# Three instead of four additions per step on GpSimd in a decoder scan kernel; slots 16 and 17 become two sums of TensorE

## The chip, the cores and the metric

The kernel runs on one core of one Trainium2 chip. The metric is the time of one execution on the device in microseconds (us), the median of several runs. The core has four engines that compute, each with its own queue of instructions, and they meet only at semaphores: TensorE (PE; its weight loads are listed as PEld), VectorE (DVE), ScalarE (ACT) and GpSimd (POOL). SyncE (SP) only starts transfers here. An engine works through its queue in order: an instruction that waits holds up everything behind it.

## The reference, cut to what matters

Sixteen sequences of 224 tokens and 512 features go through a Mamba layer, a pooled cross layer and a mixture of eight experts, with a layer norm after each. The change touches only the recurrence of the first layer:

```
deltaA = exp(delta[..., None] * A)
deltaBu = delta[..., None] * Bm[:, :, None, :] * xc[..., None]
# scan over the tokens, for 1024 channels x 16 states
h = dA * h + dBu
y = einsum('bdn,bn->bd', h, c)          # sum over the 16 states
y = (y + xc * Dp) * silu(z)
```

## The kernel before, in words

The program has three parts: a short beginning (to about 75 us), sixteen **steps**, one for each sequence (to about 1925 us), and the experts (from about 1990 us). Steps 2 to 11 are the body of a loop that does two steps a turn; steps 0, 1 and 12 to 15 are written out.

A step cuts the recurrence of one sequence into 32 **slots**: eight blocks of 128 channels (KB) times four groups of four states (Q). A slot is a tile of 128 channels by 4 states by 224 tokens = 128x896. Each slot passes through these instructions:

- POOL, L954: the input u = dx * B, written into a buffer of the ring `u`.
- ACT, L806: four exponentials, the decays, into one of two PSUM halves (`ring`).
- DVE, L1235: the scan. For 25 slots its result stays in `ring`; for the seven slots of POOLED = (1, 5, 9, ..., 25) it goes into the slot's buffer of `u`.
- the product with C: DVE, L1244, for the 25 slots; POOL, L959, for the seven. POOL does the product of slot s behind the L954 of slot s + 2.
- PE, L1540: the **sum** of a slot, four matmuls of the product with the identity, which add the four states into the PSUM bank of y. The trace shows a float32 matmul as two records, so a sum is "x8" there.

For the slots in ADDED POOL does one thing more: behind the product of slot s it adds the product of slot s - 1 into it (L965). PE then leaves out slot s - 1 and does one sum for both:

```
if s + 1 in ADDED:                                        # L1536, PE
    return
product_made(pe, b, s)
...
last.then_inc(sum_done, 2 if s in ADDED else 1)           # L1542
```

The ring `u` has five buffers up to slot 19 and four from slot 20 on (`s % 5 if s < 20 else s % 4`). POOL may write slot s (L954) only when PE has summed the slot that had this buffer before; it waits for `sum_done` (L949). So slot 21 waits for the sum of slot 16, slot 22 for that of 17, slot 25 for that of 21, slot 26 for that of 22, slot 27 for that of 23, slot 30 for that of 26. Before the change slot 16's buffer is given back only by the shared sum of 16 and 17.

Beside the 32 slots each engine does **side work** of the neighbouring sequences: PE projects the next sequence (L1368; a group "x24" is twelve matmuls of it), projects its time steps (L1379: dt0 to dt3), forms outputs (L1391, L1407, L1415), patches (L1423) and routing; ACT turns dt3 into terms (L579 to L584) of which DVE makes a correction (L1078, corr3); POOL makes the time steps (L888 to L895), normalised rows (L939), context (L933) and the scatter (L921). Tables (PE_AT, DVE_AT, ...) name the slot behind which each part stands. On PE, behind slot 15 stand twelve projection matmuls of the next gate (z0 and half of z1); behind slot 17 the patches (L1423); behind slot 20 twelve more projection matmuls and a transposition; behind 21 dt2; behind 25 dt3. DVE gets to corr3 behind the scan of slot 28.

Of the kernel before, what the change touches and what calls it, by code (L numbers as in the profile page):

```python
# [14 lines left out]
def build_decoder(nc, t):  # L15
# [42 lines left out]
    with ctx:  # L58
# [191 lines left out]
        def apart(eng):  # L250


            eng.sem_inc(wait_kept, 1)
# [89 lines left out]

        POOLED = tuple(range(1, SLOTS - Q, 4))
        MADE = SLOTS - len(POOLED)
        ADDED = (5, 9, 13, 17)
        made = lambda s: s + 1 - sum(p <= s for p in POOLED)
        pooled = lambda s: sum(p <= s for p in POOLED)

# [530 lines left out]
        def _(pool):  # L880
# [63 lines left out]
            def body(b, par):  # L944
                def main(s):
# [10 lines left out]
                    if s - 2 in POOLED:  # L956
                        q = (s - 2) % Q
                        pool.wait_ge(scan_done, b * SLOTS + (s - 1))
                        nc.gpsimd.tensor_tensor(u[:, u_of[s - 2]], u[:, u_of[s - 2]], bc[:, 1, q * QN:(q + 1) * QN, :], ALU.mult  # L959
                                                ).then_inc(pooled_ready if s - 2 not in ADDED else multiplied, 1)  # L960
                    if s - 2 in ADDED:
                        pool.wait_ge(multiplied, b * len(ADDED) + (ADDED.index(s - 2) + 1))
                        apart(pool)
# [377 lines left out]
        def _(pe):  # L1341
# [185 lines left out]
            def body(b, par):  # L1527
                def main(s):
# [3 lines left out]
                    if q == 0:  # L1532
                        if k % 2 == 0:
                            pe.wait_ge(skip_ready, b * PAIRS + (k // 2 + 1))
                            apart(pe)
                    if s + 1 in ADDED:  # L1536
                        return
                    product_made(pe, b, s)
                    for i in range(QN):
                        last = nc.tensor.matmul(o, ident, u[:, u_of[s], i, :], start=False, stop=(q == Q - 1 and i == QN - 1),  # L1540
                                                skip_group_check=True)
                    last.then_inc(sum_done, 2 if s in ADDED else 1)  # L1542

# [149 lines left out]
```

## Time and profile before

| what | value |
|---|---|
| time, median of 3 runs | 2677.05 us (2675.32 to 2677.08) |
| the profiled execution's own time | 2675.47 us |
| its span, first to last instruction | 2673.7 us |
| busy in the span | PE 2429.7, PEld 2054.5, DVE 2122.7, POOL 1786.1, ACT 1753.4 us |
| mean granted clock of TensorE | 0.954 |

Busy time is the time in which the engine had an instruction running. In a group of rows, "[0.57 <-POOL arena L959]" behind an instruction says that its engine sat idle for 0.57 us just before it, and that this instruction of POOL ended last of what it waited for. Records of matmuls overlap a little, so the distance from one start to the next tells more than a duration. PEclk is the granted clock as a share of full speed. "issue" is time in which the profile shows no wait.

### The profile page before, as it was taken

The numbers are of one execution on the slowest core, as the hardware profiler recorded it, in microseconds if no ns is written. First come the engines' busy times: TensorE is split into PE (matmuls) and PEld (weight loads), VectorE is DVE, ScalarE is ACT, GpSimd is POOL, SyncE is SP. The second block draws the span as 40 slices with busy tenths as digits, with TensorE's granted clock in tenths as the row PEclk, the third lists the DMA queues.
The fourth block names the chain that finished last, engine by engine and source line by source line (L and its number), as shares of the span: only waits on it lengthen the run. The fifth ranks groups of instructions, "written<-read, shape, count | busy, mean of one in ns | idle before, by whom it ended". The sixth has DMA issues, their size and how long they took to land.

```text
span 2673.7 us, 36163 instructions
## 1 busy us (share of the span) xinstructions
PE 2429.7 (91%) x11168; PEld 2054.5 (77%) x11168; DVE 2122.7 (79%) x2360; ACT 1753.4 (66%) x4011; POOL 1786.1 (67%) x1044
## 2 busy tenths in 40 slices
PE   5588999999999999999999999996869999999997
PEld 5576877777787787877777787774649999989896
DVE  5898999999999999999999999998733444444442
ACT  4676888888888887888888778887543333333331
POOL 0798999999999999999999999998610100000100
PEclk8799999999999999999999899998879999999998
DMA  7114202022120211202022120211052333333420
GB/s 226 62 49 154 80 12 90 15 84 76 29 88 19 83 47 59 87 12 91 15 83 74 31 87 18 76 42 56 25 173 95 122 131 119 122 121 125 142 81 18
DMA packets 90922, 208.63 MB, mean 78 GB/s; under 512 B 7743, under 2 KB 16575, under 8 KB 90499
## 3 DMA queue, kind: packets, MB, share of 16 engines
q1 hardware_dynamic: 81506, 184.61, 21.3%
q0 software_dynamic: 5120, 14.21, 1.7%
q10 hardware_dynamic: 4096, 7.34, 0.9%
q8 instruction: 103, 1.69, 0.3%
q14 instruction: 97, 0.79, 0.1%
HBM read 176.69 MB, written 29.98 MB: 77 GB/s over the span
## 4 chain that ended last, share of the span: by engine, by line
PE 36%; POOL 31%; issue 16%; DVE 12%; DMA 3%; ACT 1%; POOLq 0%; DVEq 0%; SPq 0%; ACTq 0%
POOL arena L954 20%; PE work L1555 12%; PE ring L1555 11%; POOL arena L959 6%; PE y L1540 5%; DVE ring L1235 4%; PE work L1368 3%; DVE arena L1070 2%; DVE arena L1244 2%; PE work L1391 1%; PE work L1407 1%; POOL arena L965 1%; POOL arena L892 1%; POOL arena L890 1%; POOL arena L888 1%
## 5 line engine op out<-in xcount | busy, mean ns | idle before, releaser
L954 POOL TENSOR_TENSOR arena<-arena 128x896 f32<-128x896 f32 x512 | 1058.3, 2089 | 56.8 <-PE y L1540 41.4
L806 ACT ACTIVATE ring<-arena,small 128x224 f32<-128x224 f32 x2048 | 795.4, 436 | 190.0 <-DVE arena L1244 150.4
L1540 PE MATMUL y<-arena,cst_sb 128*128 128x224 f32 x3584 | 779.7, 370 | 113.9 <-POOL arena L965 67.4
L1235 DVE TENSOR_TENSOR_SCAN ring<-ring,arena 128x896 f32<-128x896 f32 x400 | 809.4, 2024 | 57.9 <-POOL arena L954 39.6
L1540 PEld LDWEIGHTS y<-arena,cst_sb 128*128 128x128 f32 x3584 | 696.9, 199 | 192.0 <-POOL arena L965 75.4
L978 POOL DMA_INDIRECT out<-res,ids x32 | 44.7, 1395 | 642.0 <-DVE mst L1292 559.5
L1368 PE MATMUL work<-arena 128*128 128x224 f32 x1984 | 421.2, 370 | 19.8 <-DVE arena L1070 13.3
L1244 DVE TENSOR_TENSOR arena<-ring,arena 128x896 f32<-128x896 f32 x400 | 433.4, 1083 | 5.5
L1368 PEld LDWEIGHTS work<-arena 128*128 128x128 f32 x1984 | 393.6, 201 | 33.2 <-DVE arena L1070 17.8
L1307 DVE SCALAR_TENSOR_TENSOR hidden_lo<-work,hidden_hi 128x448 fp32r<-128x448 f32 x128 | 80.0, 625 | 345.8 <-ACT hidden_hi L856 345.8
L856 ACT ACTIVATE hidden_hi<-work 128x448 fp32r<-128x448 f32 x128 | 69.7, 544 | 370.3 <-PE work L1555 370.3
L1235 DVE TENSOR_TENSOR_SCAN arena<-ring,arena 128x896 f32<-128x896 f32 x112 | 225.7, 2015 | 21.4 <-POOL arena L954 15.5
L959 POOL TENSOR_TENSOR arena<-arena 128x896 f32<-128x896 f32 x112 | 233.7, 2087 | 13.0 <-DVE arena L1235 12.8
L1391 PE MATMUL work<-arena 128*112 128x512 f32 x496 | 220.6, 593 | 0.0
L1555 PE MATMUL ring<-hidden_hi,weights_hi 128*128 128x448 f32 x512 | 190.0, 371 | 0.0
L1555 PE MATMUL work<-xe_hi,weights_hi 128*128 128x448 f32 x512 | 188.4, 368 | 1.3 <-DVE xe_lo L1270 1.3
L1555 PE MATMUL work<-xe_lo,weights_hi 128*128 128x448 f32 x512 | 188.0, 367 | 0.0
L1555 PE MATMUL work<-xe_hi,weights_lo 128*128 128x448 f32 x512 | 187.9, 367 | 0.0
L1555 PE MATMUL ring<-hidden_hi,weights_lo 128*128 128x448 f32 x512 | 187.6, 366 | 0.0
L1555 PE MATMUL ring<-hidden_lo,weights_hi 128*128 128x448 f32 x512 | 187.5, 366 | 0.0
L1391 PEld LDWEIGHTS work<-arena 128*112 128x112 f32 x496 | 88.1, 178 | 102.4 <-issue 101.7
L1257 DVE TENSOR_TENSOR weights_lo<-weights,weights_hi 128x2048 fp32r<-128x2048 f32 x64 | 146.1, 2286 | 1.2 <-ACT weights_hi L820 1.2
(194 smaller groups left out, 3340.8 us busy)
## 6 DMA issues: line engine op xcount, KB each, us to landing
weights<-in_w SPq DMA_DIRECT2D x64, 1024.0 KB, 7.1
arena<-bc_rows SPq DMA_DIRECT2D x128, 448.0 KB, 4.4
arena<-in_ctx SPq DMA_DIRECT2D x16, 896.0 KB, 5.8
expert_rows<-x2e SPq DMA_DIRECT2D x1, 7224.0 KB, 31.8
xrow<-expert_rows SPq DMA_DIRECT2D x8, 903.0 KB, 12.0
arena<-in_xT SPq DMA_DIRECT2D x16, 448.0 KB, 6.3
arena<-in_x SPq DMA_DIRECT2D x16, 448.0 KB, 3.6
out<-arena ACTq DMA_DIRECT2D x32, 224.0 KB, 2.3
```

The lines of the kernel that those rows point to most:

```text
L806: last = nc.scalar.activation(decays[s % 2][:, i * L:(i + 1) * L], delta[:, k, :], ACT.Exp, scale=a_neg[:, n:n + 1])
L856: nc.scalar.activation(r32(h_hi[:, f % HR, :]), h_bank[f % 2][:, 0:CAP], ACT.Relu).then_inc(hid_hi, 1)
L954: nc.gpsimd.tensor_tensor(u[:, u_of[s]], dx[:, k:k + 1, :].to_broadcast([P, QN, L]), bc[:, 0, q * QN:(q + 1) * QN, :], ALU.mult).then_inc( ...
L959: nc.gpsimd.tensor_tensor(u[:, u_of[s - 2]], u[:, u_of[s - 2]], bc[:, 1, q * QN:(q + 1) * QN, :], ALU.mult).then_inc(pooled_ready if s - 2 ...
L1235: nc.vector.tensor_tensor_scan(states, h, u_flat[:, u_of[s], :], 0.0, ALU.mult, ALU.add).then_inc(scan_done, 1)
L1244: nc.vector.tensor_tensor(u[:, u_of[s]], h.rearrange("p (n l) -> p n l", n=QN), bc[:, 1, q * QN:(q + 1) * QN, :], ALU.mult).then_inc(p_rea ...
L1257: nc.vector.tensor_tensor(r32(lo), w, hi, ALU.subtract).then_inc(ready, 1)
L1307: nc.vector.scalar_tensor_tensor(r32(h_lo[:, f % HR, :]), h_bank[f % 2][:, 0:CAP], 0.0, h_hi[:, f % HR, :], ALU.max, ALU.subtract).then_in ...
L1368: last = nc.tensor.matmul(bank[:, i * L:(i + 1) * L], w_in[:, c, o:o + P], xn[:, c, :], start=(c == 0), stop=(c == DC - 1))
L1391: last = nc.tensor.matmul(bank[0:H, 0:D], gate[:, 1 - par, k, h * H:(h + 1) * H], w_out[:, k, :], start=(k == 0), stop=(k == KB - 1))
L1540: last = nc.tensor.matmul(o, ident, u[:, u_of[s], i, :], start=False, stop=(q == Q - 1 and i == QN - 1), skip_group_check=True)
L1555: last = nc.tensor.matmul(out, r32(a), r32(b), start=(first and k == 0), stop=(stop and k == n - 1))
```

## The change

ADDED loses its last member. POOL no longer adds slot 16 into slot 17; PE sums slot 16 and slot 17 one after the other, each from its own buffer, and each sum gives its own buffer back. Nothing else is edited; the products, the scans and the side work stay.

```diff
@@ -343,7 +343,7 @@
         POOLED = tuple(range(1, SLOTS - Q, 4))
         MADE = SLOTS - len(POOLED)
-        ADDED = (5, 9, 13, 17)
+        ADDED = (5, 9, 13)
         made = lambda s: s + 1 - sum(p <= s for p in POOLED)
         pooled = lambda s: sum(p <= s for p in POOLED)
```

PE, around slot 16 of a step that is written out (the sum of slot 15 and twelve projection matmuls stand first; L1423 are the patches behind slot 17, and the last row holds the sums of 18, 19 and 20):

```order
 L1540 MATMUL y<-arena,cst_sb 128x224 x4
 L1368 MATMUL work<-arena 128x224 x12
-L1540 MATMUL y<-arena,cst_sb 128x224 x4
+L1540 MATMUL y<-arena,cst_sb 128x224 x8
 L1423 MATMUL work<-cst_sb,mask_b 112x224 x2
 L1540 MATMUL y<-arena,cst_sb 128x224 x12
```

Behind the projection stands one sum more, four matmuls; everything behind it on PE comes four matmuls later.

POOL in the same part of a step, before (L954 x4 are slots 16 to 19, L959 and L965 product and addition of slot 17, the next L954 x4 slots 20 to 23, L959 the product of slot 21, L921 the scatter):

```order
L954 TENSOR_TENSOR arena<-arena 128x896 x4
L959 TENSOR_TENSOR arena<-arena 128x896
L965 TENSOR_TENSOR arena<-arena 128x896
L954 TENSOR_TENSOR arena<-arena 128x896 x4
L959 TENSOR_TENSOR arena<-arena 128x896
L954 TENSOR_TENSOR arena<-arena 128x896
L921 DMA expert_rows<-x2e,slot_i 3584x516 x2
```

and after:

```order
L954 TENSOR_TENSOR arena<-arena 128x896 x4
L959 TENSOR_TENSOR arena<-arena 128x896
L954 TENSOR_TENSOR arena<-arena 128x896 x4
L959 TENSOR_TENSOR arena<-arena 128x896
L954 TENSOR_TENSOR arena<-arena 128x896
L921 DMA expert_rows<-x2e,slot_i 3584x516 x2
```

One addition is gone between slot 19's and slot 20's input; the order is otherwise the same. The queues of DVE and ACT are unchanged.

## Rows read from the trace of the kernel before

**Rows 1.** The page: the chain that ended last, by engine.
```profile
PE 36%; POOL 31%; issue 16%; DVE 12%; DMA 3%; ACT 1%; POOLq 0%; DVEq 0%; SPq 0%; ACTq 0%
```
**Rows 2.** Windows of step 8 and step 9: length, busy (count) by engine, PEclk, DMA, GB/s.
```profile
1006.50:1118.60 112.10, 105.52 (x485) 86.86 (x484) 109.17 (x120) 92.86 (x225) 106.76 (x64) 0.98 0.18 55
1118.60:1235.00 116.40, 110.93 (x497) 90.39 (x497) 111.04 (x119) 96.30 (x240) 110.52 (x64) 0.97 0.19 61
```
**Rows 3.** Groups by line, whole span: busy, mean ns of one, idle before.
```profile
L1540 PE MATMUL y<-arena,cst_sb 128*128 128x224 f32 x3584 | 779.7, 370 | 113.9 <-POOL arena L965 67.4 <-DVE arena L1244 29.6 <-POOL arena L959 13.0
...
L965 POOL TENSOR_TENSOR arena<-arena 128x896 f32<-128x896 f32 x64 | 133.4, 2084 | 14.5 <-POOL arena L959 14.3 <-DVE arena L1244 0.2
```
**Rows 4.** Waits, whole span: us in total, times, longest.
```profile
POOL arena L954 <- PE y L1540: 41.4, 45, 3.2
DVE ring L1235 <- POOL arena L954: 39.6, 29, 8.3
```
**Rows 5.** Timeline of POOL, step 8: start, us, what [idle before]; slots 17, 21-23, 25-27.
```profile
1074.26 2.08 POOL L965 TENSOR_TENSOR arena<-arena 128x896 f32<-128x896 f32 x1 [0.24 <-POOL arena L959]
...
1078.63 6.19 POOL L954 TENSOR_TENSOR arena<-arena 128x896 f32<-128x896 f32 x3 [0.24 <-PE y L1540]
...
1091.31 6.18 POOL L954 TENSOR_TENSOR arena<-arena 128x896 f32<-128x896 f32 x3
```
**Rows 6.** Timeline of PE, step 8: projection, sum 17, patches, sums 22-23, sum 25.
```profile
1072.22 4.81 PE L1368 MATMUL work<-arena 128*128 128x224 f32 x24 [0.16 <-DVE slot_i L1140]
1076.87 1.68 PE L1540 MATMUL y<-arena,cst_sb 128*128 128x224 f32 x8
1078.38 0.92 PE L1423 MATMUL work<-cst_sb,mask_b 112*112 112x224 f32 x4
...
1091.18 3.29 PE L1540 MATMUL y<-arena,cst_sb 128*128 128x224 f32 x16
...
1099.59 1.78 PE L1540 MATMUL y<-arena,cst_sb 128*128 128x224 f32 x8 [0.57 <-POOL arena L959]
```
**Rows 7.** Timeline of DVE: first scan of step 9, and its corr3.
```profile
1118.60 2.03 DVE L1235 TENSOR_TENSOR_SCAN ring<-ring,arena 128x896 f32<-128x896 f32 x1 [1.09 <-POOL arena L954]
...
1219.17 0.60 DVE L1078 SCALAR_TENSOR_TENSOR arena<-arena,work 128x448 f32<-128x448 f32 x1
```
**Rows 8.** Timeline of PE, step 9: projection, sum 17, sums 22-23.
```profile
1186.09 4.81 PE L1368 MATMUL work<-arena 128*128 128x224 f32 x24
1191.30 1.78 PE L1540 MATMUL y<-arena,cst_sb 128*128 128x224 f32 x8 [0.40 <-POOL arena L965]
...
1205.72 3.29 PE L1540 MATMUL y<-arena,cst_sb 128*128 128x224 f32 x16
```
**Rows 9.** Timeline of POOL, step 9: the addition, then slots 20-23.
```profile
1189.16 2.08 POOL L965 TENSOR_TENSOR arena<-arena 128x896 f32<-128x896 f32 x1 [0.24 <-POOL arena L959]
1191.20 8.23 POOL L954 TENSOR_TENSOR arena<-arena 128x896 f32<-128x896 f32 x4
```
**Rows 10.** Timeline of ACT, step 9: the last term of dt3.
```profile
1218.55 0.54 ACT L584 ACTIVATE arena<-work 128x448 f32<-128x448 f32 x1
```
**Rows 11.** Timeline of POOL, step 1: slot 25.
```profile
288.27 2.09 POOL L954 TENSOR_TENSOR arena<-arena 128x896 f32<-128x896 f32 x1 [1.47 <-PE y L1540]
```
**Rows 12.** Timeline of PE, step 0: projection behind slot 15, sum 20.
```profile
151.22 4.70 PE L1368 MATMUL work<-arena 128*128 128x224 f32 x24
...
163.18 1.78 PE L1540 MATMUL y<-arena,cst_sb 128*128 128x224 f32 x8 [0.49 <-DVE arena L1244]
```
**Rows 13.** Timeline of DVE, step 15: scans 20 and 30.
```profile
1884.85 2.03 DVE L1235 TENSOR_TENSOR_SCAN ring<-ring,arena 128x896 f32<-128x896 f32 x1 [1.48 <-POOL arena L954]
...
1912.72 2.03 DVE L1235 TENSOR_TENSOR_SCAN ring<-ring,arena 128x896 f32<-128x896 f32 x1 [0.36 <-POOL arena L954]
```
**Rows 14.** Timeline of PE, step 3: the projection behind slot 15.
```profile
499.60 6.08 PE L1368 MATMUL work<-arena 128*128 128x224 f32 x24
```
**Rows 15.** Timeline of POOL, step 3: slots 21-23.
```profile
507.28 6.18 POOL L954 TENSOR_TENSOR arena<-arena 128x896 f32<-128x896 f32 x3 [3.19 <-PE y L1540]
```

## The prediction

> **What bounds the kernel now.** I read the page's chain first, then windows by step, then who waits for whom, then the engines' timelines around slots 16 to 27 of two neighbouring steps. The chain gives 36% to PE, which also has the experts, and 31% to POOL [rows 1]; within the steps most of it runs over POOL. Taken alone that says: POOL is the bound, take work from it. The windows say something narrower: in step 8 (112.1 us) DVE is busy 109.2, POOL 106.8 and PE 105.5 us [rows 2]. No engine has 7 us to spare, and PE, where the work goes, is as full as POOL, where it comes from. So the question is which wait ends last at the place of the change, and who is late behind it. Both directions of waiting exist: POOL's L954 waited 41.4 us for sums of PE in all, and the scans that write ring waited 39.6 us for POOL [rows 4].
>
> **What goes and what comes.** Sixteen additions go, one a step. An addition is 2.08 us, with a wait of 0.24 for POOL's own product before it [rows 3, 5]: 2.3 us a step on POOL, 37 us in all. Sixteen sums come, four matmuls each. Behind the projection the sum of 17 starts at 1076.87 and the next instruction at 1078.38 [rows 6]: 1.51 us a step on PE, 24 us in all. These are the outer bounds: from -37 (POOL's saving arrives whole and PE's work is hidden) to +24 (the reverse), the low clock aside. DVE and ACT do nothing new, and no transfer moves. PE's wait for the product of slot 16 adds nothing: DVE makes it before PE has finished the projection.
>
> **A step of the first kind, step 8.** The new sum of 16 stands exactly where the shared sum stood: behind the projection that starts at 1072.22. It starts at 1076.87 and ends at 1078.38, and POOL's slot 21 starts at 1078.63, 0.25 later [rows 5, 6]. Before, POOL came to that place at 1078.39 and waited 0.24. Now it comes 2.3 us earlier and waits 2.5, for the same instant. The projection waited for DVE (slot_i), not for the addition, so nothing pulls PE forward. POOL's saving in this step is 0.
>
> PE now has the sum of 17 still to do, so everything behind is 1.51 late. Who notices? Slot 26 needs the sum of 22. Sums 22 and 23 start at 1091.18 [rows 6]; that of 22 ends 1.51 later, at 1092.7. With the delay and 0.25 of latency slot 26 can start at 1094.45. Slot 25 starts at 1091.31 and slot 26 follows 2.05 behind [rows 5], at 1093.36. So POOL is 1.1 late from slot 26 on. So is the product of slot 25 behind slot 27, for whose sum PE already waits (0.57) [rows 6]; PE has no slack left there. The lateness reaches the next step: its first scan at 1118.60 already waits 1.09 for POOL [rows 7]. Loss: 1.1 us.
>
> Eight steps are of this kind by POOL's timeline, in that slot 21 waits for PE: 3, 4, 6, 8, 10, 11, 12, 13. 8 x 1.1 = +8.8.
>
> **A step of the second kind, step 9.** Here PE finishes the projection (1186.09 and 4.65 from start to start, as in step 8: 1190.74) before the addition ends and waits 0.40 for it; POOL's slot 21 stands 2.05 behind 1191.20, at 1193.25, without a wait [rows 8, 9]. Now the sum of 16 runs 1190.74 to 1192.25, and slot 21 starts at 1192.5: 0.75 gained. PE ends both sums at 1193.8, against 1192.9 before (1191.30 and some 1.6): 0.9 late. By slot 26 this has eaten the gain: sums 22 and 23 start at 1205.72 [rows 8], so slot 26 can start at 1205.72 + 1.51 + 0.9 + 0.25 = 1208.4, and before it started at 1207.96. POOL is 0.4 late, then the product of slot 25, its sum, dt3, and the terms of dt3 that ACT makes. DVE's corr3 starts at 1219.17 right behind the last of these, 1218.55 + 0.54 [rows 7, 10]. It has no slack, so DVE ends the step 0.4 late too, though it was 0.75 ahead at slot 21. Five steps: 2, 5, 7, 9, 14. 5 x 0.4 = +2.0.
>
> **The edges.** Step 1 is of the first kind, but slot 25 waits 1.47 for PE already [rows 11]; PE's delay arrives whole: +1.5. In step 0 PE has no outputs, and its sum of slot 20 waits for DVE [rows 12]. After the projection (from 151.22, 4.65 long) four sums (6.1) fit in before 162.0, where it stood at 163.18: -1.2. In step 15 there is no next sequence and PE waits for POOL. The sum of 16 is done long before slot 21 asks for it, and DVE gets its waits for POOL back: four of them, the first 1.48 (scan 20), the last 0.36 (scan 30) [rows 13], the two between 0.38 and 0.37. Together -2.6.
>
> **Sum.** 8.8 + 2.0 + 1.5 - 1.2 - 2.6 = +8.5 us. The profiled execution took 2675.5 us, of which 1.8 lie outside the span; with the change 2684.0. The median of the runs is 1.6 us above that execution: 2685.6. I forecast **2685 us**, slower by 0.3%.
>
> **A rule that speaks against this.** PE's loads are busy 86.9 of the 112.1 us of step 8, DVE 109.2 [rows 2]. The Trainium skill, "Perfetto Trace Analysis", section Identifying the Most-Contended Engine, says to judge TensorE's room by the busy share of its weight loads, not by that of its matmuls, and the other engines by occupancy. By that rule PE has over 20% to spare, the added sum is hidden, and DVE and POOL are the contended ones: less work on POOL is free or a gain. That is rival B or A below. The stretch in question is against it: from 1072.22 to 1078.38 PE goes from one instruction to the next without a gap [rows 6], and its share over the whole step says nothing of that place.
>
> **Rivals.**
>
> A: POOL is the bound, as the chain suggests, and its 2.3 us a step arrive. DVE can gain no more than it waits for POOL: about 1.1 a step in the middle [rows 7], 39.6 for all scans into ring [rows 4]. For it: the chain. Against it: slot 21 hangs on PE's projection, which the change does not move. It would give 1.1 to 1.3 x 16, some 20 us: 2657.
>
> B: no change. PE's added 1.5 us is taken up by its waits before slot 26 and 30, slots 26 and 27 are not late, and the edges (-3.8) meet step 1 (+1.5) and small losses. It decides where PE has over 1.5 us of idle time between slots 17 and 22; step 8 shows none there. 2674 to 2681.
>
> C: slower, by the clock. The same twelve matmuls of projection that take 4.81 us in step 8 take 6.08 in step 3, part of them at 1.2 GHz instead of 2.4, and slot 21 waits 3.19 instead of 0.24 [rows 6, 14, 15]. This happens in three steps, 3, 10 and 12. If the new rhythm puts such a dip there in five steps more, that is 3 us each: +15 on the +8.5, 2700. For it: POOL and PE wait for each other at new places. Against it: PE has fewer gaps than before.
>
> D: faster, by the clock. Fuller PE, dips gone from those three steps (-9), and shorter ones elsewhere: 8.5 - 9 - 8 = -8, 2669. The granted clock is 0.98 and 0.97 in steps 8 and 9 [rows 2], so there is only this much to get back. The Trainium skill, "TensorE: Matmul & The Clock Gate", Part 1, says that it is idle time that halves the clock and activity that restores it; by that D is likelier than C, but the place of each dip can't be worked out from the rows.
>
> **Chances.** Forecast 0.50; A 0.07; B 0.27; C 0.11; D 0.05. What can be told from no change here is about 0.2%, 5.4 us. Faster by more: A, D: 0.12. Within: B, and a little of the forecast's lower end: 0.30. Slower: 0.58. The range for 8 in 10 takes in B and most of C and D: 2670 to 2697; the forecast's own is 2680 to 2691.
>
> **What would show it.** Right: in the middle steps slot 21 of POOL waits about 2.5 us for a sum; slot 25 to 27 start to wait for PE; slot 26 of the first kind is 1.1 later against slot 21; the scans' wait for POOL at the start of a step stays or grows; L1540 has 3712 records. Two neighbouring steps take 230 us (228.5 before). Wrong: two steps take under 228 us, POOL does not wait at slot 21, or PE's dips stand elsewhere and their sum is larger than 8 us. Step 15 should be 2.6 shorter whatever the others do.

## The result and the profile after

| | before | after |
|---|---|---|
| time, median of 7 runs each | 2674.80 us (2671.73 to 2677.08) | 2685.95 us (2684.64 to 2687.69) |
| ratio, 95% interval | | 1.0044 [1.0033, 1.0055] |
| the profiled execution's own time | 2675.47 us | 2686.33 us |
| its span | 2673.7 us | 2684.5 us |
| mean granted clock | 0.954 | 0.960 |

The change costs 11.15 us, 0.4%. The forecast was 2685: +8 on the 2677.05 that three runs had given for the kernel before. Seven runs put that kernel at 2674.80.

The chain of the kernel after, by engine, against [rows 1]: PE has 2% more of the span, POOL 1% less.

```profile
PE 38%; POOL 30%; issue 13%; DVE 12%; DMA 3%; ACT 2%; POOLq 1%; DVEq 0%; SPq 0%; ACTq 0%
```

The groups by line of the kernel after, whole span (busy, mean ns of one, idle before), against [rows 3]: 128 matmul records and 16 additions have changed sides.

```profile
L1540 PE MATMUL y<-arena,cst_sb 128*128 128x224 f32 x3712 | 795.0, 366 | 106.9 <-POOL arena L965 63.8 <-DVE arena L1244 30.9 <-POOL arena L959 9.6
L965 POOL TENSOR_TENSOR arena<-arena 128x896 f32<-128x896 f32 x48 | 100.0, 2083 | 10.6 <-POOL arena L959 10.2 <-DVE arena L1244 0.4
```

The waits of the kernel after (us in total, times, longest), against [rows 4]: POOL's wait for sums has grown by 47.1 us, more than the 33.4 us of additions that left POOL. The scans wait 10.6 us less for POOL.

```profile
POOL arena L954 <- PE y L1540: 88.5, 77, 5.4
DVE ring L1235 <- POOL arena L954: 29.0, 19, 8.3
```

Step 8 of the kernel after, POOL's timeline, against [rows 5]; the step starts at 1013.89. The rows are slot 20, slots 21 to 23, then 25, then 26 and 27 together, and 30.

```profile
1081.29 2.09 POOL L954 TENSOR_TENSOR arena<-arena 128x896 f32<-128x896 f32 x1
1085.93 6.19 POOL L954 TENSOR_TENSOR arena<-arena 128x896 f32<-128x896 f32 x3 [2.56 <-PE y L1540]
...
1099.20 2.09 POOL L954 TENSOR_TENSOR arena<-arena 128x896 f32<-128x896 f32 x1 [0.61 <-PE y L1540]
1101.86 4.14 POOL L954 TENSOR_TENSOR arena<-arena 128x896 f32<-128x896 f32 x2 [0.57 <-PE y L1540]
...
1112.63 2.09 POOL L954 TENSOR_TENSOR arena<-arena 128x896 f32<-128x896 f32 x1 [0.50 <-PE y L1540]
```

The same step on PE, against [rows 6]: projection, sums 16 and 17, patches, sums 18 to 20 in one unbroken row.

```profile
1079.53 4.81 PE L1368 MATMUL work<-arena 128*128 128x224 f32 x24 [0.16 <-DVE slot_i L1140]
1084.17 3.19 PE L1540 MATMUL y<-arena,cst_sb 128*128 128x224 f32 x16
1087.20 0.92 PE L1423 MATMUL work<-cst_sb,mask_b 112*112 112x224 f32 x4
1087.95 4.71 PE L1540 MATMUL y<-arena,cst_sb 128*128 128x224 f32 x24
```

Measured from the step's first scan, slot 21 starts at 72.04 (before 72.13) and slot 26 at 87.97 (before 86.86, its place in [rows 5]): 1.1 later. The next first scan follows 113.24 behind the first (112.10 before) and waits as long as in [rows 7]:

```profile
1127.13 2.03 DVE L1235 TENSOR_TENSOR_SCAN ring<-ring,arena 128x896 f32<-128x896 f32 x1 [1.10 <-POOL arena L954]
```

### The profile page after: what moved, and what is told of

Same layout as the page of the kernel before. It is cut to its first block, busy times and chain, and to the rows that moved or that the text cites. A ratio compares the mean times of both kernels' runs of the same rounds, so it can differ in the third digit from the quotient of the medians.

```text
span 2684.5 us, 36397 instructions
## 1 busy us (share of the span) xinstructions
PE 2441.4 (91%) x11296; PEld 2068.9 (77%) x11296; DVE 2123.9 (79%) x2360; ACT 1751.3 (65%) x4011; POOL 1754.0 (65%) x1028
## 4 chain that ended last, share of the span: by engine, by line
PE 38%; POOL 30%; issue 13%; DVE 12%; DMA 3%; ACT 2%; POOLq 1%; DVEq 0%; SPq 0%; ACTq 0%
POOL arena L954 17%; PE work L1555 12%; PE ring L1555 11%; PE y L1540 7%; POOL arena L959 5%; DVE ring L1235 5%; PE work L1368 4%; DVE arena L1244 2%; POOL arena L892 2%; POOL arena L890 2%; POOL arena L888 2%; DMA arena<-bc_rows 2%; POOL arena L965 1%; DVE arena L1025 1%; PE work L1379 1%
## 5 line engine op out<-in xcount | busy, mean ns | idle before, releaser
L954 POOL TENSOR_TENSOR arena<-arena 128x896 f32<-128x896 f32 x512 | 1058.9, 2088 | 101.2 <-PE y L1540 88.5
L1540 PE MATMUL y<-arena,cst_sb 128*128 128x224 f32 x3712 | 795.0, 366 | 106.9 <-POOL arena L965 63.8
L1540 PEld LDWEIGHTS y<-arena,cst_sb 128*128 128x128 f32 x3712 | 715.1, 197 | 181.9 <-POOL arena L965 70.2
L959 POOL TENSOR_TENSOR arena<-arena 128x896 f32<-128x896 f32 x112 | 233.8, 2088 | 14.9 <-DVE arena L1235 14.9
L1391 PE MATMUL work<-arena 128*112 128x512 f32 x496 | 220.5, 592 | 0.0
L1391 PEld LDWEIGHTS work<-arena 128*112 128x112 f32 x496 | 87.8, 177 | 102.5 <-issue 101.9
```

The source lines that it names most:

```text
L954: nc.gpsimd.tensor_tensor(u[:, u_of[s]], dx[:, k:k + 1, :].to_broadcast([P, QN, L]), bc[:, 0, q * QN:(q + 1) * QN, :], ALU.mult).then_inc( ...
L1391: last = nc.tensor.matmul(bank[0:H, 0:D], gate[:, 1 - par, k, h * H:(h + 1) * H], w_out[:, k, :], start=(k == 0), stop=(k == KB - 1))
```

## All steps, and the clock

The table gives the length of each step, first scan to first scan (of step 15, to its last scan), from DVE's timeline, for two executions of each kernel. They are the profiled ones and one more each ("again"), the further executions at the end of the experiments.

| | 0 | 1 | 2 | 3 | 4 | 5 | 6 | 7 | 8 | 9 | 10 | 11 | 12 | 13 | 14 | 15 |
|---|---|---|---|---|---|---|---|---|---|---|---|---|---|---|---|---|
| before | 114.1 | 116.6 | 114.4 | 118.7 | 112.0 | 116.7 | 112.0 | 116.5 | 112.1 | 116.4 | 114.8 | 113.9 | 118.1 | 113.7 | 112.7 | 113.3 |
| before, again | 114.9 | 116.7 | 114.0 | 117.9 | 113.7 | 116.4 | 114.9 | 115.6 | 113.7 | 116.2 | 114.8 | 113.9 | 114.0 | 114.9 | 112.8 | 113.2 |
| after | 113.2 | 115.7 | 116.7 | 119.8 | 113.2 | 116.9 | 116.1 | 117.1 | 113.2 | 119.7 | 113.3 | 115.1 | 116.1 | 117.8 | 113.5 | 109.1 |
| after, again | 114.0 | 115.8 | 116.8 | 118.3 | 116.1 | 116.9 | 113.3 | 119.8 | 113.3 | 116.9 | 116.2 | 115.1 | 114.9 | 116.1 | 114.8 | 109.7 |

The loop's even steps are at best 112.0 long before and 113.2 after. The odd ones 5, 7 and 9 go from about 116.5 to 116.9 (in the 116.5 the clock has a part too: see "The second kind" below). On top of that come steps in which TensorE's clock is low just before slot 21, on the sum of slot 15 and the projection behind it. In step 9 of the kernel after, PE's timeline reads:

```profile
1186.16 3.29 PE L1540 MATMUL y<-arena,cst_sb 128*128 128x224 f32 x16 [1.38 <-POOL arena L965]
1190.86 1.02 PE L1379 MATMUL work<-dbl,w_dt_sb 33*128 33x224 f32 x4 [1.40 <-DVE arena L1078]
...
1193.12 3.33 PE L1540 MATMUL y<-arena,cst_sb 128*128 128x224 f32 x8
1196.25 6.01 PE L1368 MATMUL work<-arena 128*128 128x224 f32 x24
1202.10 3.19 PE L1540 MATMUL y<-arena,cst_sb 128*128 128x224 f32 x16
```

The sum of 15 takes 3.33 us where in step 8 it takes 1.76, the projection 6.01 where it takes 4.81. POOL's slot 21 shows the bill:

```profile
1203.86 6.20 POOL L954 TENSOR_TENSOR arena<-arena 128x896 f32<-128x896 f32 x3 [5.23 <-PE y L1540]
```

It waits 5.23 instead of 2.56, and the step is 119.7 long instead of 116.9. In these two kernels a fully slow projection (over 5.5 us) so costs 2.8 (in an even step 114.8 - 112.0 before and 116.1 - 113.2 after). In a half slow step the low clock lies on the sum of slot 15 and the projection itself takes its usual 4.7 to 4.8 us; slot 21 waits 1.2 to 1.5 us more than undisturbed, and the step is about 1.3 longer. Full ones by the rows: before in steps 3, 10, 12, again in 6 and 10; after in 3, 6, 9, 13, again in 4, 7, 10. Half ones: before again 13; after 12, again 3, 13, 14.

A third disturbance stands earlier. Between 20 and 32 us of most steps the clock is low for a while at no cost. Where it stays low longer there, POOL waits 1.7 us for a sum at 32 to 34 us, and the step is about 1.6 longer: before in step 12, again in 3, 4 and 8; after in step 2, again in 2. So the 113.7 of steps 4 and 8 in the second row of the table is not an undisturbed length; no even step of the loop is undisturbed in that execution.

## The experiments

Times are medians; ratios are to the kernel before on the same chip, with a 95% interval.

**The addition gone, no sum in its place.** PE leaves slot 16 out (y lacks it), waits for its product all the same, and gives both buffers back behind the sum of 17.

```diff
-                    if s + 1 in ADDED:
+                    if s + 1 in ADDED or s == 16:
                         return
+                    if s == 17:
+                        product_made(pe, b, 16)
...
-                    last.then_inc(sum_done, 2 if s in ADDED else 1)
+                    last.then_inc(sum_done, 2 if s in ADDED or s == 17 else 1)
```

> POOL's saving alone: the addition of slot 17 is gone, and PE still does one sum there, that of slot 17 (it waits for both products and gives both buffers back). Slot 16 is left out of y. Theory (slot 21 hangs on PE's projection, so POOL's 2.3 us a step are not worth anything in steps of the first kind): slot 21 waits about 2.5 us for PE, steps 4 and 8 keep their 112.0 to 112.1 us, the steps in which PE waited for the addition gain 0.4 to 0.8 each, step 0 up to 2, step 15 2.6 or more: 5 to 10 us faster than before. Rival A (POOL is the bound, its saving arrives): step 4 and 8 lose 1 us or more each, some 20 us faster in all.

Measured 2664.29 us (2664.14 to 2669.33), ratio 0.9963 [0.9949, 0.9976]. POOL's saving alone is worth 10 us, not 20. Step 10 is 112.02 long, as undisturbed steps were before. Its POOL timeline (the step starts at 1236.54):

```profile
1308.62 6.18 POOL L954 TENSOR_TENSOR arena<-arena 128x896 f32<-128x896 f32 x3 [1.29 <-PE y L1543]
```

Slot 21 starts at 72.08, the instant of before, and there is no wait at slots 25 to 27. In undisturbed odd steps (115.7 long) it brings 0.7. The rest is at the edges: steps 0, 1 and 15 are 1.8, 0.5 and 4.4 shorter than in the profile before. The profiled execution is the slowest of the five (2669.33), and its steps 2 to 14 are together no shorter than before (1493.1 against 1492.0), since four of them have a fully slow projection; what the other four executions, 5 us faster, have in its place is not on record.

**The sum added, the addition kept.** PE sums slot 16 as well, though POOL has added it into 17 (y holds it twice); slot 21 waits for POOL's addition too.

```diff
-                    if s + 1 in ADDED:
+                    if s + 1 in ADDED and s != 16:
                         return
...
-                    last.then_inc(sum_done, 2 if s in ADDED else 1)
+                    last.then_inc(sum_done, 2 if s in ADDED and s != 17 else 1)
```

> PE's cost alone: POOL adds slot 16 into slot 17 as before, and PE sums slot 16 as well, from its own buffer (so y holds slot 16 twice). Slot 21 waits for the sum of slot 16 as in the changed kernel. Theory (what is behind the added sum on PE is late, slots 25 to 27 of POOL wait for it): steps 4 and 8 are 1.1 to 1.2 us longer than before, slots 25 and 26 wait about 0.6 us each; 10 to 15 us slower than before, so some 3 us slower than the changed kernel, whose gains at the edges are missing. Rival B (PE takes the sum up in its idle time): within 2 us of before. If the loss of the changed kernel came from POOL's wait of 2.5 us at slot 21, this kernel, in which POOL comes to slot 21 as late as before, would not be slower.

Measured 2699.87 us (2686.66 to 2704.73), ratio 1.0087 [1.0064, 1.0110]: +25, more than the 10 to 15 I had set down. Both single changes have a price of their own: -10 and +25, together +15, against +11 for the whole change. The waits of slots 25 and 26 that the change brought stand here with the addition kept. In step 7:

```profile
994.37 2.08 POOL L958 TENSOR_TENSOR arena<-arena 128x896 f32<-128x896 f32 x1 [0.35 <-PE y L1544]
997.02 4.12 POOL L958 TENSOR_TENSOR arena<-arena 128x896 f32<-128x896 f32 x2 [0.57 <-PE y L1544]
```

So they come from the added sum, not from the missing addition.

The steps without a disturbance are as long as in the changed kernel: 117.0 and 116.9 for steps 5 and 9 (116.9 there), 115.1 for step 11 (115.1). The 14 us above it lie at the edges, which are 5.7 us longer than in the changed kernel, and in the clock. No even step of 2 to 14 is undisturbed: in 2, 4, 12 and 14 the clock is low before slot 21; in 6, 8 and 10 it is low at the first sum of the step, which takes 3.28, 3.02 and 3.02 us where it takes 1.78 in the changed kernel, behind a wait of 2.4 us for DVE instead of some 1.0. So the 1.1 to 1.2 expected of steps 4 and 8 can't be read here (they are 117.5 and 115.2 long), and the +25 is not the price of the sum alone.

**The projection one slot later.** The changed kernel with the twelve matmuls behind slot 16 instead of 15, so that the sum of 16 stands ahead of them.

```diff
-                 "rank": 14.01, "z0.0": 15, "z0.1": 15.01, "z1.0": 15.02, "plug": 17, ...
+                 "rank": 14.01, "z0.0": 16, "z0.1": 16.01, "z1.0": 16.02, "plug": 17, ...
```

> The changed kernel, with the twelve projection matmuls of PE moved from behind slot 15 to behind slot 16, so that the sum of slot 16 is done before them. Theory: slot 21 no longer waits, but PE does as much work as before up to the sum of 17 and beyond it (its 0.15 us idle before the projection are used up by the sum), so slots 25 to 27 still wait: steps 4 and 8 take 112.8 to 113.2 us against 113.2 of the changed kernel, 2 to 6 us faster than it in all, still slower than before. Rival (the wait at slot 21 is the loss): POOL gets its 2.3 us back, steps of 111 us, 15 us or more faster than the changed kernel and faster than before.

Measured 2687.07 us (2682.94 to 2688.40), ratio 1.0045 [1.0031, 1.0058]: the same as the changed kernel. The wait moves by a slot. Step 10 (from 1250.2), POOL, slots 22, 25 and 26:

```profile
1323.56 2.09 POOL L954 TENSOR_TENSOR arena<-arena 128x896 f32<-128x896 f32 x1 [0.98 <-PE y L1540]
...
1335.31 2.08 POOL L954 TENSOR_TENSOR arena<-arena 128x896 f32<-128x896 f32 x1 [0.92 <-PE y L1540]
1337.97 4.14 POOL L954 TENSOR_TENSOR arena<-arena 128x896 f32<-128x896 f32 x2 [0.57 <-PE y L1540]
```

Undisturbed even steps take 113.0 and 112.8 (10 and 6), as expected, but the 2 to 6 us did not come: steps 2 to 14 are together 1.7 shorter than in the changed kernel, and step 1 is 3.7 longer (119.4), for a reason that is not traced. The rival, that slot 21's wait is the loss, would have given steps of 111. What costs is the amount of PE's work between slot 15 and slot 26, and that is the same in either order.

**The addition of slot 13 dropped instead of that of 17.** The same trade, 16 additions against 16 sums, four slots earlier.

```diff
-        ADDED = (5, 9, 13)
+        ADDED = (5, 9, 17)
```

> Also three additions a step, but the one left out is that of slot 13 instead of 17; PE sums 12 and 13. At slot 13 PE waited 1.3 us for the addition in every middle step, so the sum of slot 12 fits there for 0.2 us net. Theory: the same number of matmuls and additions as in the changed kernel costs nothing here, POOL gains little because slot 21 still hangs on PE's projection: 3 to 12 us faster than before, steps 4 and 8 at 111.5 to 112.3 us. Rival D' (PE's added work is what costs, wherever it stands): slower than before by 5 us or more, as in the changed kernel.

Measured **2658.60 us** (2655.72 to 2660.75), ratio 0.9941 [0.9928, 0.9954]: faster than both kernels, 16 us below the one before and 27 below the changed one. Before, PE stood idle at this place in step 8:

```profile
1061.88 0.60 PE L1352 MATMUL work<-cst_sb,arena 112*128 112x112 f32 x4
1063.85 3.29 PE L1540 MATMUL y<-arena,cst_sb 128*128 128x224 f32 x16 [1.36 <-POOL arena L965]
1068.55 1.02 PE L1379 MATMUL work<-dbl,w_dt_sb 33*128 33x224 f32 x4 [1.41 <-DVE arena L1078]
```

1.36 us for the shared sum of 12 and 13, then 1.41 for a correction of DVE's. With slot 12 summed by itself, step 8 (from 999.00) reads:

```profile
1054.38 1.78 PE L1540 MATMUL y<-arena,cst_sb 128*128 128x224 f32 x8
1056.00 0.55 PE L1352 MATMUL work<-cst_sb,arena 112*128 112x112 f32 x4
1056.38 3.21 PE L1540 MATMUL y<-arena,cst_sb 128*128 128x224 f32 x16
1060.77 1.02 PE L1379 MATMUL work<-dbl,w_dt_sb 33*128 33x224 f32 x4 [1.18 <-DVE arena L1078]
```

The extra sum fills the wait for the addition, which is gone; dt1 stands at 61.77 in the step (62.05 before), the projection at 65.44 (65.72). An undisturbed even step is 111.8 long, 0.2 less than before: in the middle steps the sum is free, no more. The gain is elsewhere. Steps 0, 1 and 15 are together 10.1 us shorter; why is not traced (with the addition of 17 gone and no sum at all they are 6.7 shorter). Steps 2 to 14 are together 8.2 shorter. Steps 3, 10 and 12, whose fully slow projections are gone, are together 9.6 shorter; the slow projections of this execution (steps 7, 11 and 13, 5.6 to 5.7 us) cost slot 21 only 1.3 us. There is one profiled execution, so that the edit itself thins out the slow projections is not shown, though its six runs agree within 0.2%.

**Is it the place, or the trade?** The same trade at the other two places, and two trades at once.

```diff
-        ADDED = (5, 9, 13)
+        ADDED = (9, 13, 17)
```

> ADDED = (9, 13, 17): POOL makes the additions of slots 9, 13 and 17; slots 4 and 5 are two sums of PE. Against the kernel before: the same trade (16 additions less, 16 sums more) at another place. Theory 1 (the place decides: the extra sum costs only where PE stands on the path from the projection to slot 21; at slot 4 PE waits for POOL or DVE anyway): not slower than before, 2660 to 2675, an undisturbed even step of the loop at 111.5 to 112.2 and slot 21's wait as before (about 0.3 or somewhat more). Rival (an extra sum on PE costs about 1.1 us a step wherever it stands): 2685, steps of 113.2.

```diff
+        ADDED = (5, 13, 17)
```

> ADDED = (5, 13, 17): slots 8 and 9 are two sums of PE. Theory 1 (the place decides): not slower than before, 2660 to 2675, undisturbed even steps 111.5 to 112.2, slot 21's wait near 0.3. Rival (an extra sum costs wherever it stands): 2685, steps of 113.2.

```diff
+        ADDED = (5, 17)
```

> ADDED = (5, 17): both slots 9 and 13 lose their addition; POOL has two additions a step. Against the kernel without slot 13's alone (2658.6). Theory 1 (each of the two places has idle time of PE for one extra sum): at or below it, 2650 to 2660. Rival (the one wait of PE before the product of 13 was all the room there was): the second sum costs, 2660 to 2675.

```diff
+        ADDED = (9, 17)
```

> ADDED = (9, 17): slots 5 and 13 lose their addition. Theory 1 (room for one extra sum at each place): 2650 to 2660. Rival (room for one only): 2660 to 2675.

| additions dropped | us | ratio | POOL's wait for PE, total |
|---|---|---|---|
| none (before) | 2674.51, 17 runs | 1 | 41.4 |
| 5 | 2697.61 (2694.62 to 2706.12) | 1.0086 [1.0072, 1.0100] | 97.4 |
| 9 | 2689.59 (2686.15 to 2690.27) | 1.0054 [1.0041, 1.0068] | 90.5 |
| 13 | 2658.60 (2655.72 to 2660.75) | 0.9941 [0.9928, 0.9954] | 42.0 |
| 17 (the change) | 2685.95 (2684.64 to 2687.69) | 1.0044 [1.0033, 1.0055] | 88.5 |
| 9 and 13 | 2676.56 (2673.35 to 2681.61) | 1.0008 [0.9999, 1.0016] | 102.5 |
| 5 and 13 | 2686.72 (2683.48 to 2691.59) | 1.0044 [1.0030, 1.0058] | 89.0 |

My theory that slots 5 and 9 would be free places falls: they cost 23 and 15 us, more than slot 17. The rival, 1.1 us a step wherever the sum stands, falls too, at 13. The prices nearly add: 15 or 23 beside the -16 of slot 13 make -1 and +7, measured +2 and +12. Slot 13 is the one place of the four where it pays.

The totals mix three things. By an undisturbed middle step alone the places cost +2.4 us (slot 5: steps 8 and 10, 114.4 and 114.5 against 112.0), +0.8 (slot 9: step 13, 114.5 against 113.7), -0.2 (slot 13) and +1.2 (slot 17). The edges give back 9.6, 0.5, 10.1 and 6.0 us in the profiled executions. So slot 9 is cheaper than slot 17 in a middle step and dearer in all, because its edges give nothing. The low clock does the rest.

The rows show where 9 costs. Step 8 there (from 1013.95) is 114.0 long; PE, then POOL's slots 13 and 14, and 15:

```profile
1048.70 8.75 PE L1391 MATMUL work<-arena 128*112 128x512 f32 x20
1057.28 3.19 PE L1540 MATMUL y<-arena,cst_sb 128*128 128x224 f32 x16
1060.31 3.60 PE L1391 MATMUL work<-arena 128*112 128x512 f32 x8
1063.74 1.68 PE L1540 MATMUL y<-arena,cst_sb 128*128 128x224 f32 x8
...
1078.47 3.04 PE L1540 MATMUL y<-arena,cst_sb 128*128 128x224 f32 x8
1081.30 5.16 PE L1368 MATMUL work<-arena 128*128 128x224 f32 x24
```

```profile
1059.04 4.14 POOL L954 TENSOR_TENSOR arena<-arena 128x896 f32<-128x896 f32 x2 [0.79 <-PE y L1540]
1065.50 2.08 POOL L954 TENSOR_TENSOR arena<-arena 128x896 f32<-128x896 f32 x1 [2.31 <-PE y L1540]
```

Sums 8 and 9 stand behind 8.6 us of outputs (L1391) that wait for nothing; PE has no idle time to put a sum into, and POOL is already waiting for the buffers of 8 and 10. That makes POOL 0.7 us late at slot 16 (57.96 in the step against 57.25), and this is all of the 2.0 us that the place explains. The other 1.3 are the clock: the sum of 15 takes 3.04 us instead of 1.76. In this execution the clock is low there in every step from 2 to 12, and slot 21 waits 1.5 us for PE in each; in step 13, at full clock, it waits 0.3.

For slot 5 the extra sum also carries its own wait into PE's queue. Step 8 there (from 1022.99), PE, and POOL's slots 10 and 11:

```profile
1044.78 1.78 PE L1540 MATMUL y<-arena,cst_sb 128*128 128x224 f32 x8 [1.86 <-DVE arena L1244]
1046.40 0.93 PE L1352 MATMUL work<-cst_sb,x2e 112*128 112x112 f32 x8
...
1054.48 3.19 PE L1540 MATMUL y<-arena,cst_sb 128*128 128x224 f32 x16
```

```profile
1056.24 4.14 POOL L954 TENSOR_TENSOR arena<-arena 128x896 f32<-128x896 f32 x2 [3.33 <-PE y L1540]
```

PE waits 1.86 for the product of slot 4 before the side work that it used to begin at once, and slot 10 pays 3.33 us; the step is 114.4 long at full clock on the sum of 15 and the projection. (This kernel's profiled execution, 2706.12, is the slowest of its six.)

**Four buffers early, five late.** The rule of the ring turned round, once on the changed kernel, once with slot 13 dropped instead: does the end of a step need the fifth buffer?

```diff
-    u_of = [s % 5 if s < 20 else s % 4 for s in range(SLOTS)]
+    u_of = [s % 4 if s < 12 else (s - 12) % 5 for s in range(SLOTS)]
```

> The changed kernel with another ring: four buffers for slots 0 to 11 and five for slots 12 to 31 (before: five up to slot 19, four from 20 on). Slot 21 still waits for the sum of slot 16, but slots 25 to 27 wait for the sums of 20 to 22 instead of 21 to 23, and slot 30 for that of 25. Theory (the loss comes in at slots 25 to 27): those waits and the one of slot 30 go, the steps without a slow projection fall from 113.2 to 112.0 or less, 10 us or more faster than the changed kernel in all, if the early slots do not pay for their fourth buffer. Rival (PE itself is the bound of the step, POOL's waits only follow it; through dt3 and DVE's correction the loss stays): within 3 us of the changed kernel.

> Both: additions at 5, 9 and 17 (12 and 13 are two sums), and the other ring. Theory: slot 21 still hangs on the shared sum of 16 and 17, so the ring brings only the wait of slot 30 (0.5 us a step): 2650 to 2657, 2 to 8 us faster than with the change of the slot alone. Rival (the early slots with four buffers wait for PE's outputs): slower than with the slot alone.

Measured 2740.77 us, ratio 1.0240 [1.0226, 1.0255], and 2743.18 us, ratio 1.0248 [1.0234, 1.0263]. The waits at slots 25 to 27 are gone, but the early slots now wait in each step. On the first of the two, step 8 (from 1043.77), slots 8 and 12:

```profile
1073.94 8.24 POOL L954 TENSOR_TENSOR arena<-arena 128x896 f32<-128x896 f32 x4 [2.00 <-PE y L1540]
...
1088.70 2.09 POOL L954 TENSOR_TENSOR arena<-arena 128x896 f32<-128x896 f32 x1 [2.14 <-PE y L1540]
```

Part of the loss is the clock again: in this step PE waits 2.77 and 2.67 us ahead of the shared sum of 12 and 13, and that sum then takes 5.63 us instead of 3.29. The early part needs the fifth buffer more than the late part; what a fifth late buffer alone is worth stays open.

**Each kernel once more**, for the clock.

> The kernel before, once more, for its trace. If the places of TensorE's clock dips are set by the program, the slow projection behind slot 15 (over 5.5 us) stands in steps 3, 10 and 12 again and every step has its length within 0.3 us. If they wander from run to run, other steps have it, and the rest keep their lengths.

> The changed kernel, once more, for its trace. Theory: steps with an undisturbed projection take 113.2 (even) again; whether the slow projection stands in steps 3, 6, 9 and 13 again tells whether the 2 to 3 us that the two profiles differ by beyond the forecast are the change's or the run's.

2676.09 and 2687.74 us. Their steps are in the table above. The slow projections stand in other steps, and their number is similar. Undisturbed lengths that both executions of a kernel have are the same to 0.1 us (after: 113.2 and 113.3, 116.9 and 116.9; before: 113.9 in step 11).

## Why the prediction was right

**Step 8.** Every instant came as worked out: slot 21 waits 2.56 (2.5 forecast) and starts when it did, slot 26 is 1.1 later, slots 25 to 27 wait for PE, and the loss reaches the next step. The undisturbed step is 1.2 longer (1.1 forecast). The addition alone (112.02) and the whole change (113.2) split it: saving 0, sum 1.2.

**The second kind.** Slot 21 starts at 73.9 in step 5 or 11 where it stood at 74.65 in step 9 before ([rows 9]: 2.05 behind 1191.20): the 0.75 of the forecast. Slot 26 is at 89.8, before at 89.36: the 0.4. The odd steps grew by 0.5. The addition alone gives 0.7 there, the sum takes back 1.2.

What makes a step one of the second kind, the prediction did not see: it is the clock. In steps 2, 5, 7, 9 and 14 of the profile before, and in no other of 2 to 14, the shared sum of 12 and 13 runs slow and makes POOL 1 us late for slot 17. The first row shows that sum in step 9 of the profile before, the second POOL's slot 21 in step 7 of the further execution, where the sum takes 3.29:

```profile
1177.72 4.98 PE L1540 MATMUL y<-arena,cst_sb 128*128 128x224 f32 x16 [1.31 <-POOL arena L965]
...
968.13 6.18 POOL L954 TENSOR_TENSOR arena<-arena 128x896 f32<-128x896 f32 x3 [0.21 <-PE y L1540]
```

That step 7 is of the first kind, and 115.6 long instead of the 116.5 that the same step took in the first execution. In the further execution the second kind is steps 5, 9, 12 and 14. After the change the same slow sum costs 0.2 at most (step 4 is 113.2 with it, step 8 without), because POOL would wait for PE at slot 21 anyway. So at full clock an odd step goes from 115.6 (this one step shows it) to 116.9, and the change costs 1.2 to 1.3 in an even or odd step; the 0.4 of the forecast holds for a step that the low clock had already made longer.

**The sum over steps 2 to 14** came out too low. It was +10.8; the two profiles show +16.6 (1508.6 against 1492.0), the two further executions +15.6. What was left out is mostly the clock. In the first pair the changed kernel has one fully slow and one half slow projection more, 2.8 + 1.3 = 4.1. In the second it has one fully slow and two half slow projections more, and two of the early stretches of 1.6 fewer: 2.2. This is rival C at a quarter of its size or less. It did not decide the sign, since the 10.8 stand without it. The rest, 1.7 and 2.6 us, is in the lengths themselves: 1.2 instead of 1.1 in the first kind, 0.5 and more instead of 0.4 in the second. That the added sum causes these dips is not shown: the addition alone has four full ones (steps 2, 8, 11 and 12) and is still faster than before.

**Step 1** had the wrong sign. Its slot 25 does wait 1.5 longer, as forecast (2.99 against the 1.47 of [rows 11]), yet the step is 0.9 shorter in both pairs. PE comes to the projection 2.3 us earlier in the step. In the profile before, the sum of 15 ran at a low clock there, and POOL waited before slot 15; both are gone:

```profile
254.86 2.08 POOL L954 TENSOR_TENSOR arena<-arena 128x896 f32<-128x896 f32 x1 [0.66 <-PE y L1540]
...
267.00 3.35 PE L1540 MATMUL y<-arena,cst_sb 128*128 128x224 f32 x8
```

(The first row is POOL's, the second PE's, both of before.) In the further pair PE comes to the projection 1.6 us earlier, though before the sum of 15 ran at full clock there (1.78); POOL's wait before slot 15 was 0.26. I took the step's state at slot 15 as unchanged; at an edge it is not. What makes step 1 start better is not traced. The error is 2.4 us.

**Step 15** gave 4.2 and 3.5 us where 2.6 were forecast. The four waits of [rows 13] are gone, as said (the last of them stands before the scan of slot 29, not 30). Another 0.5 is won before slot 19 in the first pair only, and 0.6 (0.4 in the further pair) between the scans of 30 and 31, where DVE in the profile before waits 0.48 for PE and after does not. **Step 0** gave 0.9 in both pairs (1.2 forecast).

So the total was right by luck in part: two errors of opposite sign. On the mean of the two pairs the middle steps cost 5.3 more than forecast, and the edges gave 3.4 more (-5.7 against -2.3, step 1 the most of it). Net +10.4 from first to last scan, forecast +8.5. That 2685 lies so near 2685.95 has a further part of luck: on the 2674.80 of seven runs the same +8.5 makes 2683.3.

**The rivals.** A, POOL's saving arrives, is refuted: with no sum at all in its place it is 10 us, and nothing of it in even steps. B, PE's work hidden, is refuted by the waits of slots 25 to 27 and by the 113.2 of undisturbed steps. D did not occur as a gain: the mean granted clock did rise, from 0.954 to 0.960 (0.959 in the further execution), but slow projections, full and half, went from 3 to 5, and from 3 to 6 in the further pair. (The prediction calls D likelier than C in one sentence and gives C the larger chance, 0.11 against 0.05; the runs lean the way of the chances.)

**The rule on room.** The weight loads are busy 88.3 of the 113.2 us of step 8, 22% idle, and over the span 2068.9 of 2684.5. The Trainium skill, "Perfetto Trace Analysis", section Identifying the Most-Contended Engine, judges TensorE by that share. Here the share said nothing on the question: the same 24 us of matmuls cost between -16 and +23 us by place.

## What to carry to other kernels

When work moves from one engine to another that is nearly as full, the price is read slot by slot: look for an idle time of the receiving engine that ends on the very work that is dropped. At slot 13 PE waited 1.36 us for the addition, and a sum of 1.51 put there in its stead cost nothing in a middle step; at the three other places, where PE ran without a gap or the extra sum brought its own wait along, it cost 0.8 to 2.4 us a step. The totals, -16 against +11 to +23, hold the first and last steps and the low clock as well, so try the same trade at every place the table allows before judging it. Compare only steps that ran at the same clock: a slow sum of 15 alone made slot 9 look like 2.0 us a step where the place costs 0.7 to 0.8. And read the first and last steps for themselves: their state at the place of the change is not the one of before.

## What was unexpected in the hardware

The same idle times of PE do not always bring a low clock. In steps 8 and 9 of the kernel after PE waits 1.28 and 1.40, and 1.38 and 1.40 us, ahead of the sum of 15, and only in step 9 does the clock fall. Windows of these stretches of the kernel after (length, busy and count by engine, granted clock as a share of 2.4 GHz, DMA share, GB/s), step 8 twice, step 9 twice. The last two rows are the stretch from 24 to 32 us of the two steps:

```profile
1069.00:1079.40 10.40, 7.68 (x42) 6.23 (x40) 10.22 (x15) 8.55 (x22) 10.37 (x6) 1.00 0.15 44
1079.40:1087.20 7.80, 7.67 (x41) 7.66 (x42) 7.76 (x7) 5.51 (x14) 5.24 (x3) 1.00 0.02 4
1184.00:1196.20 12.20, 9.42 (x42) 8.14 (x41) 12.12 (x16) 10.22 (x26) 12.17 (x6) 0.83 0.13 39
1196.20:1205.00 8.80, 8.80 (x41) 8.51 (x41) 6.99 (x8) 4.38 (x12) 3.34 (x3) 0.85 0.00 1
...
1037.90:1045.90 8.00, 8.00 (x34) 7.37 (x33) 7.90 (x13) 7.04 (x20) 7.72 (x4) 0.79 0.10 30
1151.10:1159.10 8.00, 6.75 (x42) 6.40 (x43) 7.89 (x13) 7.30 (x20) 7.09 (x4) 1.00 0.09 29
```

The two steps differ in what came earlier; that this is the cause is not shown. In step 8 the clock was low between 24 and 32 us (0.79), where it costs nothing; in step 9 it was not (1.00). In both executions of the changed kernel each of the steps 2 to 14 has a low clock at one of the two places and none has it at both. Before, only step 12 of the first execution has both. It is no rule of the kernel, though: with the addition of 9 dropped, steps 2 to 12 all have both.

In which steps the dips stand changes from one execution of the same kernel to the next. With the additions of 9 and 13 dropped, the slow stretch moves against the step little by little. In steps 4, 6 and 8 the projection takes 5.04, 5.07 and 5.55 us and the sum of 15 before it 3.15, 3.12 and 2.64. What one gains the other loses: slot 21 starts at 73.96 or 73.97 in each, and the steps are 113.9 to 114.0 long. So the projection's own duration does not tell what a slow stretch costs; the instant of slot 21 does. Steps must be compared among those whose sum of 15 and projection both ran at full clock.
